# A negated row minimum in place of a row maximum and its rescale, in a fused attention and MLP kernel

## The reference

```python
scale = 1.0 / math.sqrt(NOPE + ROPE)                     # 192 ** -0.5
scores = jnp.einsum('bhqd,bhkd->bhqk', q, k) * scale
scores = jnp.where(causal[None, None], -jnp.inf, scores)
probs = jax.nn.softmax(scores.astype(jnp.float32), axis=-1)
attn = jnp.einsum('bhqk,bhkd->bhqd', probs, v)
attn = attn + io                                         # io: a small side branch, one row per head
out = attn.transpose(0, 2, 1, 3).reshape(B, S, NH * VD) @ W_o
x = _layernorm(x + out)
x = _layernorm(x + ffn(x))    # three ternary weight matrices of 1024 x 256, silu(up) * gate, down
```

## Time and profile before

| | before |
|---|---|
| median of three runs | 735.93 us |
| the profiled execution, its own time | 736.02 us |
| its span, first to last instruction | 734.2 us |
| PE busy | 667.7 us (91%) |
| DVE busy | 491.5 us (67%) |
| ACT busy | 397.2 us (54%) |
| POOL busy | 365.4 us (50%) |

### The profile page before, as it was taken

The page is one execution under the profiler, slowest core; times in us unless marked ns, Lnnn a source line. Parts: engine busy times, 40 slices in busy tenths (PEclk is TensorE's granted clock), DMA queues, the critical chain, the costliest instruction groups (busy, mean ns, idle before and its releaser), DMA issues.

```text
span 734.2 us, 14324 instructions
## 1 busy us (share of the span) xinstructions
PE 667.7 (91%) x4496; PEld 604.6 (82%) x4496; DVE 491.5 (67%) x1421; ACT 397.2 (54%) x940; POOL 365.4 (50%) x313
## 2 busy tenths in 40 slices
PE   5567799999999999999999999999999999897895
PEld 5557699888988898889888988898889887787895
DVE  2665366666766676667666766666666677995895
ACT  3251344765475647564756465656565658544552
POOL 5622344835474548344844474457435634530563
PEclk9875599999999999999999999999999999999998
DMA  6153210451036103610361037103610382000000
GB/s 199 47 143 79 58 51 1 109 129 51 1 87 151 50 0 88 148 50 0 86 150 50 0 86 150 50 0 86 150 50 0 86 228 73 2 1 1 1 30 30
DMA packets 28720, 50.52 MB, mean 69 GB/s; under 512 B 8976, under 2 KB 19472, under 8 KB 28688
## 3 DMA queue, kind: packets, MB, share of 16 engines
q1 hardware_dynamic: 28688, 50.12, 27.3%
HBM read 15.50 MB, written 1.05 MB: 23 GB/s over the span
## 4 chain that ended last, share of the span: by engine, by line
PE 57%; DVE 16%; ACT 11%; issue 9%; POOL 4%; SPq 1%; DMA 0%; ACTq 0%; DVEq 0%; POOLq 0%
PE J L676 10%; PE J L678 9%; PE J L677 9%; DVE PTl L1059 4%; PE J L702 4%; ACT kvraw L1023 3%; PE SC L693 3%; PE SC L690 3%; PE SC L691 3%; PE SC L692 3%; ACT Pb L960 3%; PE SC L689 3%; POOL rstd L608 3%; DVE SC L1122 3%; ACT PTh L942 2%
## 5 line engine op out<-in xcount | busy, mean ns | idle before, releaser
L1059 DVE TENSOR_TENSOR PTl<-J,PTh 128x512 fp32r<-128x512 f32 (+1 forms) x192 | 102.2, 552 | 69.5 <-ACT PTh L942 68.9
L960 ACT ACTIVATE Pb<-SC,nm 128x128 f32<-128x128 f32 (+7 forms) x128 | 94.7, 740 | 56.3 <-DVE nm L1126 56.1
L1122 DVE CUSTOM_DVE_ANT_0 SC<-SC,mask 128x128 f32<-128x128 f32 (+7 forms) x128 | 97.3, 760 | 27.6 <-PE SC L693 25.3
L676 PE MATMUL J<-PTh,Vh 128*128 128x256 f32 x320 | 89.0, 278 | 6.8 <-DVE PTl L1059 6.7
L942 ACT ACTIVATE PTh<-J 128x512 fp32r<-128x512 f32 (+1 forms) x192 | 87.3, 492 | 10.4 <-PE J L702 9.6
L702 PE MATMUL J<-ident,Pb 128*128 128x128 f32 x576 | 88.2, 280 | 5.2 <-ACT Pb L960 5.1
L677 PE MATMUL J<-PTl,Vh 128*128 128x256 f32 x320 | 90.2, 282 | 0.0
L678 PE MATMUL J<-PTh,Vl 128*128 128x256 f32 x320 | 90.0, 281 | 0.0
L702 PEld LDWEIGHTS J<-ident,Pb 128*128 128x128 f32 x576 | 64.4, 142 | 12.4 <-ACT Pb L960 5.3
L676 PEld LDWEIGHTS J<-PTh,Vh 128*128 128x128 f32 x320 | 61.0, 191 | 12.3 <-DVE PTl L1059 9.2
L689 PE MATMUL SC<-KNh,QNh 128*128 128x512 f32 (+1 forms) x192 | 69.3, 361 | 0.0
(11 more groups left out here) (268 smaller groups left out, 1935.9 us busy)
## 6 DMA issues: line engine op xcount, KB each, us to landing
KD<-RKh SPq DMA_DIRECT2D x32, 256.0 KB, 4.5
KL<-RKl SPq DMA_DIRECT2D x32, 256.0 KB, 5.0
KX<-KX SPq DMA_DIRECT2D x16, 256.0 KB, 2.3
QX<-QX SPq DMA_DIRECT2D x16, 256.0 KB, 2.4
QS<-RQh SPq DMA_DIRECT2D x16, 256.0 KB, 3.9
QS<-RQl SPq DMA_DIRECT2D x16, 256.0 KB, 4.5
r_kv<-in_L_attn_W_ckv SPq DMA_DIRECT2D x8, 384.0 KB, 3.4
r_qn<-in_L_attn_W_qT SPq DMA_DIRECT2D x16, 128.0 KB, 2.7
```

Source lines behind the costliest of these rows:

```text
L676: mm(o, lhsT=wh, rhs=xh, start=start, stop=False)
L960: act.activation(Pb[i % 2][:, w], SC[i % 2][:, w], ACT.Exp, bias=nm[:, i % 2:i % 2 + 1], scale=SCALE, accum_out=sm[:, b, i:i + 1]).then_in ...
L1059: dve.tensor_tensor(o, i, h.bitcast(F32), ALU.subtract).then_inc(done[kind], 1)
L1122: dve.tensor_tensor_reduce(out=SC[i % 2][:, w], in0=SC[i % 2][:, w], in1=mask[:, 128 * (7 - i):S], scale=1.0, scalar=LOW, op0=ALU.add, op1 ...
```

## The change

The reduction's own scale factor, which was 1.0, becomes `-SCALE`, and it reduces by minimum instead of maximum. The in-place scores are therefore already scaled and negated, and the row value read out of the accumulator is `-SCALE * max`, which is `nm` itself. The third DVE instruction, its wait, the semaphore `mx_ready` and the small tile `mx` go. ACT's exponential takes the factor -1.0 in place of `SCALE`. The side branch's own softmax (`smx`) stays as it was.

```diff
-LOW = -3.0e38
+LOW, HIGH = -3.0e38, 3.0e38
...
-        mx = sb("mx", [128, 2])
         nm = sb("nm", [128, 2])
...
-        mx_ready, nm_ready = sem("mx_ready"), sem("nm_ready")
+        nm_ready = sem("nm_ready")
...
                         act.activation(Pb[i % 2][:, w], SC[i % 2][:, w], ACT.Exp, bias=nm[:, i % 2:i % 2 + 1],
-                                       scale=SCALE, accum_out=sm[:, b, i:i + 1]).then_inc(exp_done, 1)
+                                       scale=-1.0, accum_out=sm[:, b, i:i + 1]).then_inc(exp_done, 1)
...
                         dve.tensor_tensor_reduce(out=SC[i % 2][:, w], in0=SC[i % 2][:, w], in1=mask[:, 128 * (7 - i):S],
-                                                 scale=1.0, scalar=LOW, op0=ALU.add, op1=ALU.max,
-                                                 accum_out=mx[:, i % 2:i % 2 + 1]).then_inc(mx_ready, 1)
-                        dve.wait_ge(mx_ready, T * u + i + 1)
-                        dve.tensor_scalar(nm[:, i % 2:i % 2 + 1], mx[:, i % 2:i % 2 + 1], -SCALE, None, ALU.mult).then_inc(nm_ready, 1)
+                                                 scale=-SCALE, scalar=HIGH, op0=ALU.add, op1=ALU.min,
+                                                 accum_out=nm[:, i % 2:i % 2 + 1]).then_inc(nm_ready, 1)
```

## The result

The changed kernel takes 727.87 us, the median of six runs (724.66 to 729.12), beside 736.76 us for the kernel before in the same comparison (734.15 to 738.24). The ratio is 0.9874, with a 95% interval of 0.9854 to 0.9894: 1.3% faster, 9 us. A second measurement of it gave 727.30 us and 0.9883 (0.9854 to 0.9913). The forecast was 730.4 us with a range of 728.6 to 735.0. The direction was right, and so was the way the gain comes, through PE's waits; the gain was put at 5.7 us and is half as large again, since one step of the sum was priced wrongly.

A forecast was written before the change was run, and what follows sets the result against it. PE was taken to bound the kernel, so only its waits could shrink: 3.48 us in six iterations, 0.38 in FIRST and 1.80 in LAST, 5.66 us off 736.02, giving 730.4 us, range 728.6 to 735.0.

The forecast's parts named there:

- What bounds it: Whole kernel: PE is busy 91% of the span, so removed DVE instructions shorten the run only through PE's waits.
- places called covered: Loop: the other 13 of an iteration's 16 reductions, where ACT or DVE is held by something else, give nothing.
- The release of exponentials: Where nm releases ACT's exponential, the accumulator read itself releases it instead, 0.18 us earlier, at 12 places.
- The step from the accumulator read to the next instruction: DVE's order at tile 0: 0.30 us becomes 0.10, giving 0.20 us, between 0.12 and 0.23.
- thirteen places with a register instruction: Places in DVE's own order, in the loop, FIRST and LAST's start, with a register instruction before the next one.
- its own 31 places: The 31 of 128 reductions on the chain of waits, in FIRST, loop and LAST, together giving 5.66 us.
- the first: Rival: the step after the read stays at 0.18 us, so the gain is 4.1 us, 731.9 us; chance 0.14.
- The third place of an iteration: Second half, tile 0's nm ahead of two low parts, statistics and kvraw before the key transposes: 0.20 us.
- the forecast's sign: Loop: the PE wait before the key transposes kt, 0.47 us, would be near 0.27 if the forecast was right.
- The placement: Dropping mx moves the tiles behind it 32 bytes down in SBUF; taken as 0.
- The sum: Six iterations 3.48 us, FIRST 0.38 and LAST 1.80: 5.66 us off 736.02, so 730.4 us.
- The range's lower end: Whole run: 0.23 us at 13 places, 0.18 at six, 6.3 us in all, less a microsecond of scatter: 728.6.

The follow-up runs named there:

- Tile 7 alone: The change made only for query tile 7 of each head, tiles lying as before, against the kernel before: 733.50 us, ratio 0.9974.
- the run with the wait alone: The changed kernel plus a DVE wait on nm_ready behind the accumulator read, no third instruction: 731.73 us, ratio 0.9947 against the kernel before.
- the one with the short instruction alone: The changed kernel, mx kept, plus an unrelated 128x1 multiply behind the accumulator read without waiting on it: 728.79 us, ratio 0.9905 against the kernel before.
- the kernel with early statistics: The changed kernel with the next pair's key and value statistics merged one place earlier: 725.54 us, ratio 0.9874 against the kernel before.

## Why the prediction was wrong

**What bounds it: right.** The gain came through PE's waits in the loop and along DVE in LAST. Of the places called covered, one in the loop wasn't (below).

**The release of exponentials, 0.18 us each: right.** Tile 7 alone gives 0.15 an iteration; the row of ACT shows 0.36 becoming 0.17.

**The step from the accumulator read to the next instruction: wrong, and this is the step that failed.** The forecast bounded it between 0.07 and 0.18 us and took 0.10, from ACT's own read. It is 0.00. The bounds came from rows of other instruction pairs, and the lower one was no bound: that the step from `nm` to its follower is 0.07 says how long `nm` holds DVE, not how long a read does. So the whole step of before goes, where 0.10 was counted as left. That step was 0.30 us at the head of an iteration, but 0.27 ahead of the key transposes (419.74 - 419.47) and 0.25 in FIRST and in LAST; the forecast had read the 0.30 into all thirteen places with a register instruction. At its own 31 places this makes 12 x 0.18 + 6 x 0.30 + 6 x 0.27 + 7 x 0.25 = 7.3 us and 728.7, which is 1.7 of the 2.5 us by which the forecast missed. The run with the wait alone and the one with the short instruction alone show it from both sides. None of the rivals had it; the first leaned the other way and fell.

**The places.** The third place of an iteration gave its 0.27 us, 0.22 of it at the first key transposes, and nothing at the wait that carries the idle mark. There the forecast's sign, 0.27 instead of 0.47, failed, though the place gave more than the 0.20 counted. A place that the chain didn't pass gave PE 0.10: tile 4 of the second head. There the late low part held only the weight load of PE's next matmul, which shows as 0.38 us instead of 0.28 for that matmul and as no wait:

```profile
437.28 0.38 PE L676 MATMUL J<-PTh,Vh 128*128 128x256 f32 x1
437.50 0.28 PE L677 MATMUL J<-PTl,Vh 128*128 128x256 f32 x1
```
```profile
433.27 0.28 PE L675 MATMUL J<-PTh,Vh 128*128 128x256 f32 x1
433.39 0.28 PE L676 MATMUL J<-PTl,Vh 128*128 128x256 f32 x1
```

(before, then after: 0.22 us from start to start, then 0.12)

**The placement: wrong at 0.** It is worth 0.13 us of an iteration, some 0.8 us in the loop.

**The sum.** FIRST 0.4 us (forecast 0.38), six iterations of 0.93 or 5.6 (3.48), LAST 2.2 (1.80): 8.2 us where 5.66 were forecast. The timed runs give 8.3 and 8.9. That the two profiled executions lie 8.4 us apart is in part chance: the 1 us of the prologue comes back while the clock rises in FIRST (0.7 us) and at one wait of the first iteration alone (0.4 us, ahead of the matmul on `Woh` and `iocol`), where PE's step is anything from 0.45 to 1.78 us in the kernels here, whatever their edit. The range's lower end, 728.6, had assumed at most 0.23 us at a place that gave 0.30, and nothing for placement.

**The rule on semaphores.** The forecast had weighed a rule of the Trainium skill, page "VectorE: DVE Perf Modes", section "The DRAIN you can't avoid": in a row of eight copies, a semaphore between two operations costs nothing extra. For a wait on an accumulator read this case measures the opposite: 0.07 us for the instruction, 0.17 to 0.29 for the wait. The section also says that a next operation which is not held starts earlier, which the forecast left out; the steps of 0.00 us agree with that. That the copies hide what a wait costs, since each holds the engine for its own time, would fit both measurements; no run here has such a row.

**What stays open:** how the placement of tiles sets the pace of matmuls, and why the kernel with early statistics gains 0.5 us an iteration and so little in its times.

## What to carry to other kernels

A short instruction that waits on the one just ahead of it on the same engine can cost everything queued behind it more than its own length: 0.25 to 0.30 us here, where the instruction without the wait held DVE for 0.07. Look for such pairs where the low parts or evictions that PE waits for stand behind them; where a reduction can write the value in the wanted scale and sign, the pair goes. For sizing, a price from another pair of instructions is no bound: what the trace of before can't show should keep a range down to nothing. And a matmul whose recorded duration is 0.1 us above its neighbours', or which starts late without an idle mark, may have waited too: here both gave time back.

## What the runs showed of the hardware

The accumulator read of DVE (0.14 us in the records) doesn't hold the next DVE instruction: it starts at the same time to 10 ns, even with a third one 0.07 us behind. With a wait on that read the next starts 0.17 us behind the read's start, and 0.26 to 0.29 if a register instruction stands behind the wait. Moving tiles by 32 bytes changed the distance of matmul starts by 1 to 2 ns of 119, up or down. The reduction by minimum with a factor takes what the one by maximum takes, 761 and 760 ns in the mean. A weight load that PE had to wait for showed as 0.1 us more on its matmul (0.38 for 0.28) and as no wait.
